# Moving GpSimd's skewed reads of batch 1 ahead of two bias additions, and dropping one wait, in a one-core attention and mixture-of-experts kernel

## The reference

```
x = x + xattn(layernorm(x), ctx)          # autocorrelation attention, 16 heads of 32
    q = xn @ Wq + bq;  k, v = ctx @ Wk + bk, ctx @ Wv + bv   (128 rows, padded to 2048)
    c = rfft(q).real * rfft(k).real - 1j * rfft(q).imag * rfft(k).imag
    corr = irfft(c);  mean over heads;  top 15 delays;  softmax of their values
    out = (sum of v rolled by each delay, weighted) @ Wo + bo
x = x + ffn(layernorm(x))                 # shared expert (1024 wide) + 4 of 16 routed experts
    shared = silu(x @ Sg.T) * (x @ Su.T) @ Sd.T
    routed = sum over 4 chosen experts of w_e * (silu(x @ G_e) * (x @ U_e)) @ D_e
```

## Time and profile before

| | us |
|---|---|
| median of 3 runs | 1008.75 |
| lowest, highest | 1003.91, 1011.58 |
| the profiled execution | 1011.18 |
| its span | 1009.4 |
| TensorE busy in it | 996.7 (99%) |
| VectorE, ScalarE, GpSimd busy | 655.6, 380.2, 475.1 |

### The profile page before, as it was taken

The page is one execution under the profiler, slowest core; times in us unless marked ns, Lnnn a source line. Parts: engine busy times, 40 slices in busy tenths (PEclk is TensorE's granted clock), DMA queues, the critical chain, the costliest instruction groups (busy, mean ns, idle before and its releaser), DMA issues.

```text
span 1009.4 us, 21034 instructions
## 1 busy us (share of the span) xinstructions
PE 996.7 (99%) x6750; PEld 612.0 (61%) x6750; DVE 655.6 (65%) x1506; ACT 380.2 (38%) x776; POOL 475.1 (47%) x540
## 2 busy tenths in 40 slices
PE   9999999999999999999999999999999999999998
PEld 7785664444444444557787778787777544444443
DVE  4947669876288899875454555554555376676765
ACT  3626534444354543314444444444444311111111
POOL 0723512312224476755445544545444267677662
PEclk9969799999999999999999999999999999999999
DMA  9733775868663441529889888998989579999675
GB/s 349 256 117 125 270 247 160 238 169 259 188 173 132 159 131 63 156 66 249 245 253 240 248 258 238 248 249 242 235 253 241 169 232 254 315 264 300 202 228 176
DMA packets 175483, 216.93 MB, mean 215 GB/s; under 512 B 101096, under 2 KB 112232, under 8 KB 174376
## 3 DMA queue, kind: packets, MB, share of 16 engines
q1 hardware_dynamic: 151640, 136.95, 45.9%
q0 software_dynamic: 23760, 78.79, 26.7%
HBM read 123.67 MB, written 69.22 MB: 191 GB/s over the span
## 4 chain that ended last, share of the span: by engine, by line
PE 83%; DVE 9%; issue 3%; DMA 2%; ACT 1%; POOL 1%; DVEq 0%; SPq 0%; ACTq 0%; POOLq 0%
PE bank L1067 18%; PE bank L940 14%; PE bank L1130 14%; PE bank L1091 9%; PE bank L956 7%; PE bank L1143 6%; PE bank L1050 5%; PE bank L1081 2%; PE bank L715 1%; PE bank L695 1%; PE bank L792 1%; PE bank L729 1%; DVE arena L1854 1%; PE bank L734 1%; DVE arena L1568 1%
## 5 line engine op out<-in xcount | busy, mean ns | idle before, releaser
L1067 PE MATMUL bank<-arena 128*128 x1716 | 211.4, 273 | 1.0 <-issue 0.6
L940 PE MATMUL bank<-arena 128*128 128x512 f16 x888 | 204.5, 381 | 1.7 <-DMA arena<-pt_dram 1.2
L1067 PEld LDWEIGHTS bank<-arena 128*128 128x128 f16 x1716 | 162.9, 98 | 27.0 <-issue 2.1
L2138 POOL DMA_INDIRECT arena<-y_dram,arena x128 | 135.8, 1061 | 77.4 <-issue 33.7
L2081 POOL DMA_INDIRECT arena<-xr_dram,arena x143 | 139.6, 976 | 58.1 <-issue 46.6
L940 PEld LDWEIGHTS bank<-arena 128*128 128x128 f16 x888 | 88.0, 100 | 103.0 <-DMA arena<-pt_dram 1.7
L1130 PE MATMUL bank<-arena 128*128 128x512 f16 x648 | 144.1, 379 | 0.0
L1091 PE MATMUL bank<-arena 128*128 x429 | 115.4, 378 | 0.5 <-ACT arena L1400 0.5
L1950 DVE SCALAR_TENSOR_TENSOR arena<-arena 128x512 f32<-128x512 f32 x128 | 95.4, 750 | 30.7 <-DMA arena<-y_dram,arena 25.8
L1883 DVE SCALAR_TENSOR_TENSOR arena<-bank,arena 128x128 f32<-128x128 f32 x143 | 41.7, 292 | 108.9 <-ACT arena L1389 79.4
L1337 ACT ACTIVATE arena<-arena 128x512 f16<-128x512 f32 x64 | 40.3, 630 | 185.7 <-DVE arena L1615 107.9
(11 more groups left out here) (227 smaller groups left out, 1340.1 us busy)
## 6 DMA issues: line engine op xcount, KB each, us to landing
y_dram<-arena SPq DMA_DIRECT2D x143, 256.0 KB
arena<-in_x SPq DMA_DIRECT2D x8, 1024.0 KB, 12.1
xr_dram<-arena SPq DMA_DIRECT2D x16, 512.0 KB, 4.0
x_dram<-arena SPq DMA_DIRECT2D x8, 1024.0 KB, 5.7
arena<-in_gu_w SPq DMA_DIRECT2D x16, 512.0 KB, 3.5
out<-arena SPq DMA_DIRECT2D x32, 256.0 KB
arena<-x_dram SPq DMA_DIRECT2D x5, 1024.0 KB, 6.0
arena<-in_gu_w POOLq DMA_DIRECT2D x8, 512.0 KB, 4.3
```

The costliest lines, as they stand in the source:

```text
L940: last = mm(bank[half][:, :], (gu_hi_s, gu_lo_s)[wp][:, c, at:at + H], xt[:, xv * KC + kc, :], start=(n == 0), stop=(n == 3 * KC - 1))
L1067: last = mm(gate_up_bank(s, s)[:, 0:2 * H], rows[:, xv * KC + kc, :], only((gu_hi_r, gu_lo_r)[wp], e, slice(kc * 2 * H, (kc + 1) * 2 * H)) ...
L2138: pool.indirect_dma_start(out=ybuf[n % RING][:, e, :], out_offset=None, in_=y_dram[:, :], in_offset=bass.IndirectOffsetOnAxis(ap=row_of[:, ...
```

## The change

On GpSimd, the wait for block 0's low parts goes. `add_bo(6)` moves from ahead of the early skewed reads to behind the loads of weight chunk 2, and `add_bo(7)` from behind chunk 2 to behind chunk 3. The waits of the reads themselves stay. The other engines' programs are the same.

```
             add_bo(5)
-            pool.wait_ge(s_lo0, TB)
-            add_bo(6)
             pool.wait_ge(s_pte, 16)
             pool.wait_ge(s_u, 1)
             pool.wait_ge(s_mm, 28)
...
             pool.dma_start(skew_d[1][:, M:EARLY], skewed(1, 1, PTW + 1, M, EARLY)).then_inc(s_sk[1], 16)
             pool.wait_ge(s_wlo, 1)
             shared_weights_in(2)
-            add_bo(7)
+            add_bo(6)
             pool.wait_ge(s_wlo, 2)
             shared_weights_in(3)
+            add_bo(7)
             pool.wait_ge(s_pt, NB)
             pool.wait_ge(s_sk2[1], 48)
```

## The result

The changed kernel takes 1011.86 us (median of 22 executions, 1003.24 to 1020.36) against 1005.26 us for the kernel before (22 executions, 997.07 to 1012.91). The ratio is 1.0069, 95% interval [1.0042, 1.0096]: about 7 us slower, inside 1% and outside the noise. The predicted 1008.9 us, its range and "within 1%" hold for the time; the forecast that the change does nothing does not.

What follows compares the result with a forecast made beforehand. TensorE was taken as the bound, busy 996.7 of 1009.4 us. Terms of +0.2, 0 and 0 us on the median of 1008.75 us gave 1008.9 us, range 1003.5 to 1012.5.

Steps and rivals of the forecast that it cites:

- Term 1: Early reads on GpSimd: they start when the early write lands plus 0.55 us start-up; +0.2 us (-0.35 to +0.3).
- my two rows: Two GpSimd transfers that started 0.52 and 0.59 us after a DMA landing, the source of the 0.55 us start-up.
- Term 2: Additions at their new places, beside VectorE's block 1 work: at most 4.99 us against 5.0 slack; 0 (0 to +0.1 us).
- Term 3: TensorE's low-clock stretch from 115 to 126 us, taken as unchanged: 0 (-4.7 to +3.0 us).
- slower: Rival: late read start-up lengthens TensorE's stall and low-clock stretch, +3.3 us, 1012.1 us; chance 0.10.
- what would prove me wrong: Signs: reads before 103.9, line 940 wait under 0.8, no low stretch after 115 us, or TensorE waiting for line 1615.
- The port rule: In SBUF, a two-input VectorE instruction and GpSimd's reads need one port, kept for the whole instruction; surplus 0.53 us at line 1645.

Runs made afterwards that it cites:

- before_third: The kernel before, unchanged, run again for its profile alone; no time or ratio is given.
- before_again: The kernel before, unchanged, as a control and for a second profile; ratio 1.0009 [0.9975, 1.0043].
- before_fourth: The kernel before, unchanged, run once more for its profile; no time or ratio is given.
- a smaller dose: The changed kernel with add_bo(7) cut into 16 additions of 128 columns instead of 4 of 512, same place; ratio 1.0027 [0.9991, 1.0063].
- wait_removed_alone: The kernel before with the wait for block 0's low parts taken out and nothing moved; ratio 1.0085 [1.0044, 1.0126].

## Why the prediction was right in part, and wrong in part

**Term 1, the reads: right in kind.** That 0.35 us at most of 4.99 could be had was right, and that the write sets the start. I added 0.55 us of start-up; it was 100.65 - (96.12 + 4.2) = 0.33 us, so the reads moved by nothing and not by +0.2. (One of my two rows was worked out with 3.3 us, the median of two transfers; the transfer that GpSimd waited for took 3.2, so its start-up was 0.6.) TensorE's wait at line 940 for the reads was 0.9 us in the profile, under the 1.0 I gave, and in both kernels it was near 1 us in some profiles and not listed in others (before: 1.2, none, none, 1.1; after: 0.9, 1.0, none).

**Term 2, the additions' new overlap: the step that failed.** I took the worst case, 4.99 us, and it is what happened (5.0). I set it against a slack of 5.0 us, and read that slack from line 1615, which "then sat idle for 4.53 us until TensorE let line 1615 start". But TensorE was at half clock there. The same rows in before_third, where it was at full clock, and `x1_tile(2, 0)`:

```profile
117.21 0.68 DVE L1646 SCALAR_TENSOR_TENSOR arena<-arena 128x512 f16<-128x512 f32 x1
117.97 0.69 DVE L1615 SCALAR_TENSOR_TENSOR arena<-bank,arena 128x512 f32<-128x512 f32 x1
...
121.03 0.74 DVE L1568 SCALAR_TENSOR_TENSOR arena<-bank,arena 128x512 f32<-128x512 f32 x1
```

VectorE ended line 1646 at 117.89 and began line 1615 at 117.97: 0.1 us of slack, and as little in before_again (113.37 to 113.45), the other profile of this kernel without the low stretch; before_fourth, with it, had 5.48 us. A slack that the low clock had made was spent on a cost that is there at full clock. Not all of the 5.0 us reached TensorE. From the end of line 1597 to `x1_tile(2, 0)` VectorE took 121.03 - 115.65 = 5.4 us in before_third and 120.85 - 117.07 = 3.8 in the changed kernel, because it waited less for ScalarE on the way, so 1.6 us were absorbed and 3.4 were left. The stalls measured are 1.9 to 3.5 us, the smaller ones where TensorE itself came 0.9 to 1.0 us late from line 940. The term should have been +2 to +3.5 us of stall and 3 to 5 us of clock, where TensorE runs at full speed.

**Term 3, the clock: taken as untouched, and it was not.** I had priced a longer low stretch (+3.0), but hung it on the reads' start-up. What brought it was the stall at line 792. Of the rivals, "slower" had the right direction and half the size, and the wrong place: it ended at 1012.1 us on the strength of a stall that did not come. In what would prove me wrong I had named TensorE waiting for line 1615; it waited for line 1568, the third instruction behind it on VectorE.

**The port rule: right, and read too mildly.** The Trainium skill, SBUF — State Buffer, "Who interferes with whom", says that whoever has the shared port keeps it for the whole instruction and that the other side is blocked fully, and I cited it. I had drawn on what it says of two SBUF inputs; the instructions that were blocked for long are tensor_scalar, with one, which the same section names among those that can take the port. The runs agree with the lock in three kernels (5.60 us, 6.94 us for four, 5.42 us), and in a smaller dose (2.20 us). That the port is what blocks is the section's account; the traces show who waited and for how long.

**The time.** 1008.9 us against 1011.86 is inside the range. Part of the closeness is luck: the kernel before measures 1005.26 in 22 executions and not 1008.75 as in the three I started from, and the shift was 6.6 us and not 0.2.

## What to carry to other kernels

Before slack on one engine is spent, ask at what speed the engine that gives it was running: a profile taken while TensorE was at its low clock shows gaps on VectorE that are gone in the executions at full clock (4.53 and 5.48 us against 0.1 here). An instruction that is off the path itself (here a bias addition wanted 80 us later) still has to be placed where the engine that shares its port has nothing urgent; a wait that looks useless ahead of such an instruction may be what keeps the two apart, so test it by itself. A chain names only the last releaser: read the landing of what stands next before crediting the whole length of what is removed.

## What the runs showed of the hardware that I had not expected

At two places VectorE did not get in between back-to-back additions of GpSimd. One instruction waited for all four: 5.60 us for one that takes 0.5, though its record begins at 111.02 and the first addition at 111.38. The other, in wait_removed_alone, came during the fourth of eight additions (79.92 to 89.77) and waited for the rest: 5.42 us for one that takes 0.2 to 0.3. Not every kind of instruction was held up. In the same run, beside the first four additions, lines 1568, 1572 and 1579 took their usual 0.73, 0.69 and 0.38 us. In another place of the same kernel, before, VectorE's small conversions beside `add_bo(2)` to `add_bo(4)` took 1.23 to 1.32 us each, one addition per instruction, as these rows show.

```profile
46.07 1.32 DVE L1541 CAST arena<-arena 128x128 f16<-128x128 f32 x1
47.30 1.30 DVE L1542 CAST arena<-arena 128x128 f16<-128x128 f32 x1
```

And beside additions of 128 columns it was mostly GpSimd that waited, 1.43 us for a piece that takes 0.44, and VectorE lost 0.2 us in four instructions and 0.26 at line 1646 (0.94 for 0.68). What decides who gets in first was not tested.

GpSimd's start of a transfer behind a DMA's landing took 0.33 us here and about 0.6 in the rows that I had used; that difference stays open as well.
